# Counts of an edge loop: windows of 128 targets in place of spans of 256-target blocks

## What is computed

```python
# layer 0: a message for each edge, summed by its source
m = jnp.concatenate([x[row], x[col]], axis=1)
m = jax.nn.relu(m @ Wm1 + bm1)
m = jax.nn.relu(m @ Wm2 + bm2)
m_sum = jax.ops.segment_sum(m, row, num_segments=x.shape[0])
...
# layer 2: the mean over the first ten edges of each source
keep = (rank < NUM_NEIGHBORS).astype(x.dtype)
sums = jax.ops.segment_sum(x[col_s] * keep[:, None], row_s, num_segments=N)
...
# layer 3: messages scaled by the edge's weight, summed by target
agg = jax.ops.segment_sum(edge_weight[:, None] * x[src], dst, num_segments=N)
```

## Time and profile before

| what | us |
|---|---|
| median of 3 runs | 911.99 |
| lowest and highest of them | 909.75, 913.79 |
| the profiled execution | 920.58 |
| its span, first to last instruction | 918.7 |
| TensorE busy in the span | 851.9 (93%) |
| VectorE busy | 662.7 (72%) |
| ScalarE busy | 503.2 (55%) |
| GpSimd busy | 292.2 (32%) |

### The profile page before, as it was taken

One profiled execution on the slowest core, in us unless ns is written; L12 is line 12 of the kernel. 1 busy time (PEld: TensorE's weight loads), 2 busy tenths in 40 slices (PEclk: granted clock), 3 DMA queues, 4 the chain that ended last, 5 costly groups with the idle time before them and its releaser, 6 DMA issues.

```text
span 918.7 us, 18692 instructions
## 1 busy us (share of the span) xinstructions
PE 851.9 (93%) x5480; PEld 545.4 (59%) x5514; DVE 662.7 (72%) x1786; ACT 503.2 (55%) x1009; POOL 292.2 (32%) x403
## 2 busy tenths in 40 slices
PE   8899949999999999999999898899899998899898
PEld 3657728989898989898889645322242223232244
DVE  6999985767766767777677466977587776877651
ACT  6432114666656666666666674566656665566531
POOL 8040047556555556555555200012031110111000
PEclk9999979999999999999999999999999999999999
DMA  3020041121212121212122100000000000000310
GB/s 87 32 87 1 0 139 60 54 69 46 69 51 70 51 69 51 68 53 70 46 71 54 47 1 1 0 1 1 1 0 1 1 1 0 1 1 0 128 57 23
DMA packets 19145, 35.87 MB, mean 39 GB/s; under 512 B 5280, under 2 KB 11552, under 8 KB 18976
## 3 DMA queue, kind: packets, MB, share of 16 engines
q0 software_dynamic: 7104, 19.41, 7.5%
q1 hardware_dynamic: 12000, 15.95, 5.1%
HBM read 29.56 MB, written 5.79 MB: 38 GB/s over the span
## 4 chain that ended last, share of the span: by engine, by line
PE 77%; DVE 15%; ACT 4%; issue 3%; POOL 1%; DMA 0%; DVEq 0%; ACTq 0%; POOLq 0%
PE PS L1453 9%; PE PS L1309 8%; PE PS L1223 7%; PE PS L1222 7%; PE PS L1170 5%; PE PS L1438 5%; PE PS L1303 5%; PE PS L1241 5%; DVE OHd L1005 5%; PE PS L1444 4%; PE PS L1215 3%; PE PS L1353 3%; PE PS L1228 3%; PE PS L1404 2%; PE PS L1300 2%
## 5 line engine op out<-in xcount | busy, mean ns | idle before, releaser
L406 POOL DMA_INDIRECT room<-Qtab,gidx x148 | 148.3, 1002 | 96.0 <-DVE gidx L837 61.2
L556 ACT ACTIVATE OHe<-OHs,sew 128x128 bf16<-128x128 bf16 x408 | 126.7, 390 | 46.6 <-DVE OHs L947 26.2
L1005 DVE CUSTOM_DVE_ANT_0 OHd<-PS,room 128x1024 bf16<-128x1024 f32 x96 | 112.3, 1220 | 8.6 <-PE PS L1404 8.5
L420 POOL TENSOR_SCALAR KV<-room,pid 128x256 bf16<-128x256 uint8 x74 | 74.9, 1012 | 134.5 <-DVE MS L912 128.8
L567 ACT ACTIVATE m2s<-m2s 128x512 f32<-128x512 f32 x68 | 42.9, 631 | 88.2 <-DVE m2s L938 60.3
L458 POOL TENSOR_TENSOR zl<-AL,Sx 128x8 f32<-128x8 f32 x9 | 1.9, 215 | 265.1 <-DVE Sx L1005 265.1
L1222 PE MATMUL PS<-Wm,m1T 128*128 128x256 f32 x276 | 83.2, 383 | 0.0
L1223 PE MATMUL PS<-Wm,m1T 128*128 128x256 f32 x276 | 82.8, 382 | 0.0
L952 DVE TENSOR_SCALAR OHd<-iotaN,dstf 128x1024 bf16<-128x1024 f16 x136 | 74.3, 586 | 9.3 <-PE PS L1309 9.3
L912 DVE TENSOR_TENSOR MS<-PS,room 128x512 f32<-128x512 f32 x68 | 47.1, 692 | 43.1 <-PE PS L1241 42.8
L938 DVE TENSOR_TENSOR m2s<-PS,bm 128x512 f32<-128x512 f32 x68 | 47.0, 691 | 42.7 <-PE PS L1223 42.7
(11 more groups left out here) (357 smaller groups left out, 1734.4 us busy)
## 6 DMA issues: line engine op xcount, KB each, us to landing
BT<-Wtab SPq DMA_DIRECT2D x1, 4096.0 KB, 13.1
room<-Qtab,gidx POOLq DMA_INDIRECT x148
room<-Stab SPq DMA_DIRECT2D x1, 2048.0 KB
Wtab<-H SPq DMA_DIRECT2D x4, 512.0 KB, 3.8
Wtab<-cs SPq DMA_DIRECT2D x4, 512.0 KB, 3.4
Qtab<-room SPq DMA_DIRECT2D x1, 1024.0 KB, 4.4
Wn<-in_L_gnn_Wn SPq DMA_DIRECT2D x1, 1024.0 KB, 5.4
x<-in_x SPq DMA_DIRECT2D x1, 512.0 KB, 4.0
```

Source lines behind the costliest of these rows:

```text
L406: g.indirect_dma_start(out=G[:, p % SLOTS, k, :], out_offset=None, in_=Qtab, in_offset=bass.IndirectOffsetOnAxis(ap=gidx[:, p, k:k + 1], a ...
L556: a.activation(OHe[:, k, j, :], OHs[:, k, :], ACT.Copy, scale=sew[:, j, bass.ds(2 * g + k, 1)])
L1005: v.tensor_tensor_reduce(junk[n % 2], bank(4, 2), mask[:, i, :], 1.0, 2 * FAR, ALU.subtract, ALU.max, Sx[:, i, hd:hd + 1]).then_inc(S("gat ...
```

## The change

Each chunk of a pair gets a window of its own, 128 targets wide, whose first target is a multiple of 32 and which lies wholly in one half (512 targets) of the nodes. A pass then has two chunks k by one window by 1 + 3 matmuls: 8 in place of 16. Where a chunk's targets don't fit into such a window, both chunks of the pair go through the same aligned windows of 128, in as many passes as it takes. The number read for a pair now packs the source block, the place of each chunk's window in steps of 32 (five bits each), and the number of further passes (three bits). The loop variable counts targets; the second chunk's window lies `further` beyond the first's.

The places come out of the least and the greatest target of each chunk. VectorE writes them into `rngp` (target + 1, zero where there is no edge) and `sew0` (target - 1024), TensorE turns both with four transposes into bank 6 (72 pairs down, 128 edges across), VectorE takes the maximum and the minimum over the edges, works out places, wide pairs and passes in nineteen small steps on 72 x 2 values, TensorE turns the packed numbers into one row (bank 4), and one VectorE addition with GpSimd's `pblk` makes `rngi`. All but that last addition now stand ahead of the first message. TensorE's wait for `spans` moves from inside the pair loop to ahead of the first `restarted()`. Allocations are left out of the diff.

```diff
@@ -36,6 +36,8 @@
 SLOPE = 0.2
 FRAC = 1.0 / 1024.0
 HALF = 65536.0
+STEP = 32
+PLACES = N // STEP
 FAR = -1e30
 BANK = 512
 
...
@@ -393,7 +399,7 @@
-            g.tensor_scalar(pblk[:, 1, 0:NPAIR - 2], pblk[:, 0, 2:NPAIR], float(NB * NB), None, ALU.mult)
+            g.tensor_scalar(pblk[:, 1, 0:NPAIR - 2], pblk[:, 0, 2:NPAIR], float(PLACES * PLACES * NB), None, ALU.mult)
...
@@ -843,13 +848,10 @@
             link(v.tensor_copy(srcl[:], ssrc[:]))
             link(v.scalar_tensor_tensor(srcl[:], srcl[:], 1.0, valid[:], ALU.add, ALU.mult))
             v.tensor_scalar(srcl[:], srcl[:], -1.0, None, ALU.add).then_inc(S("sources_ready"), 1)
-            v.tensor_copy(paired(dstf), sdst)
-            link(v.tensor_scalar(paired(skey), sdst, 7, None, ALU.arith_shift_right))
-            link(v.tensor_copy(sew0[:], skey[:]))
-            link(v.scalar_tensor_tensor(rngp[:], sew0[:], 1.0, valid[:], ALU.add, ALU.mult))
-            v.tensor_tensor(inblk, rngp[:].unsqueeze(1).to_broadcast([P, NB, NCH]),
-                            iota[:, 1:NB + 1].unsqueeze(2).to_broadcast([P, NB, NCH]), ALU.is_equal)\
-                .then_inc(S("blocks_marked"), 1)
+            link(v.tensor_copy(paired(dstf), sdst))
+            v.scalar_tensor_tensor(rngp[:], dstf[:], 1.0, valid[:], ALU.add, ALU.mult)
+            v.scalar_tensor_tensor(sew0[:], dstf[:], float(-N), valid[:], ALU.add, ALU.mult)\
+                .then_inc(S("ends_marked"), 1)
 
             eng.wait_ge(S("sources_ready"), 1)
             for k in range(2):
@@ -866,39 +868,38 @@
                     link(v.tensor_tensor(sewv[:], sewv[:], sew[:, k, :], ALU.subtract))
             v.tensor_copy(rank[:], sew[:, 0, 0:2]).then_inc(S("weights_split"), 1)
             made = bank(5).rearrange("p (k f) -> p k f", k=2)
-            eng.wait_ge(S("blocks_counted"), 1)
-            held = bank(6, 2)[0:FEW, :].rearrange("p (u n) -> p u n", u=2)[:, :, 0:NB // 2 * NPAIR]\
-                .rearrange("p u (b g) -> p u b g", g=NPAIR)
-            for i, rank_of in enumerate((falling[0:FEW, :], iota[0:FEW, 1:NB + 1])):
-                last = v.scalar_tensor_tensor(flags.rearrange("p (u b) g -> p u b g", u=2), held, 1.0,
-                                              rank_of.unsqueeze(2).to_broadcast([FEW, NB, NPAIR])
-                                              .rearrange("p (u b) g -> p u b g", u=2), ALU.min, ALU.mult)
-                if i:
-                    last.then_inc(S("blocks_read"), 1)
-                    eng.wait_ge(S("blocks_read"), 1)
-                else:
-                    link(last)
-                link(v.tensor_reduce(rngf[:, i, :], flags.rearrange("p b g -> p g b"), AX.X, ALU.max))
+            eng.wait_ge(S("ends_across"), 1)
+            ends = bank(6)[0:NPAIR, :].rearrange("p (u k e) -> p u k e", u=2, k=2)
+            v.tensor_reduce(above[:], ends[:, 0], AX.X, ALU.max)
+            v.tensor_reduce(below[:], ends[:, 1], AX.X, ALU.min).then_inc(S("ends_read"), 1)
+            eng.wait_ge(S("ends_read"), 1)
+            link(v.tensor_scalar(least[:], below[:], float(N), float(N - 1), ALU.add, ALU.min))
+            v.tensor_scalar(steps[:], least[:], 5, None, ALU.arith_shift_right)
+            link(v.tensor_scalar(upper[:], least[:], 9, None, ALU.arith_shift_right))
+            link(v.tensor_scalar(other[:], upper[:], float(BANK // STEP), float((BANK - P) // STEP), ALU.mult, ALU.add))
+            link(v.tensor_tensor(place[:], steps[:], other[:], ALU.min))
+            link(v.scalar_tensor_tensor(other[:], place[:], float(-STEP), above[:], ALU.mult, ALU.add))
+            link(v.tensor_tensor(wide[:], other[:, 0:1], other[:, 1:2], ALU.max))
+            v.tensor_scalar(wide[:], wide[:], float(P), None, ALU.is_gt)
+            link(v.tensor_tensor(upper[:, 0:1], least[:, 0:1], least[:, 1:2], ALU.min))
+            link(v.tensor_scalar(upper[:, 1:2], upper[:, 0:1], 7, None, ALU.arith_shift_right))
+            link(v.tensor_tensor(above[:, 0:1], above[:, 0:1], above[:, 1:2], ALU.max))
+            link(v.scalar_tensor_tensor(above[:, 1:2], upper[:, 1:2], float(-P), above[:, 0:1], ALU.mult, ALU.add))
+            link(v.tensor_scalar(steps[:, 0:1], above[:, 1:2], float(P - 1), None, ALU.add))
+            link(v.tensor_scalar(steps[:, 1:2], steps[:, 0:1], 7, None, ALU.arith_shift_right))
+            v.scalar_tensor_tensor(below[:, 0:1], steps[:, 1:2], -1.0, wide[:], ALU.add, ALU.mult)
+            link(v.scalar_tensor_tensor(other[:], upper[:, 1:2].to_broadcast([NPAIR, 2]), float(P // STEP), place[:],
+                                        ALU.mult, ALU.subtract))
+            link(v.scalar_tensor_tensor(place[:], other[:], wide[:, 0:1], place[:], ALU.mult, ALU.add))
+            link(v.scalar_tensor_tensor(below[:, 1:2], place[:, 1:2], float(PLACES), place[:, 0:1], ALU.mult, ALU.add))
+            v.scalar_tensor_tensor(packed[:], below[:, 1:2], float(NB), below[:, 0:1], ALU.mult, ALU.add)\
+                .then_inc(S("packed"), 1)
             eng.wait_ge(S("gathered"), 1)
             eng.wait_ge(S("pparts_done"), 1)
             v.tensor_tensor(MS[:], made, G[:, 0, :, :], ALU.add).then_inc(S("msg_ready"), 1)
-            link(v.tensor_scalar(rngf[:, 1, :], rngf[:, 1, :], 1.0, -1.0, ALU.max, ALU.add))
-            link(v.tensor_scalar(rngf[:, 0, :], rngf[:, 0, :], -1.0, float(NB), ALU.mult, ALU.add))
-
-            link(v.tensor_tensor(rngf[:, 0, :], rngf[:, 0, :], rngf[:, 1, :], ALU.min))
-            link(v.tensor_tensor(rngf[:, 1, :], rngf[:, 1, :], rngf[:, 0, :], ALU.subtract))
-            link(v.tensor_scalar(rngf[:, 1, :], rngf[:, 1, :], 2.0, None, ALU.add))
-            link(v.tensor_copy(rngi[:], rngf[:, 1, :]))
-            link(v.tensor_scalar(rngi[:], rngi[:], 1, None, ALU.arith_shift_right))
-            link(v.tensor_copy(rngf[:, 1, :], rngi[:]))
-            link(v.tensor_scalar(nfrom[:], rngf[:, 1, :], -2.0, float(NB), ALU.mult, ALU.add))
-            link(v.tensor_tensor(nfrom[:], nfrom[:], rngf[:, 0, :], ALU.min))
-            link(v.tensor_scalar(rngf[:, 1, :], rngf[:, 1, :], 2.0, -1.0, ALU.mult, ALU.add))
-            link(v.tensor_tensor(rngf[:, 1, :], rngf[:, 1, :], nfrom[:], ALU.add))
             eng.wait_ge(S("pair_blocks"), 1)
-            link(v.tensor_tensor(rngf[:, 1, :], rngf[:, 1, :], pblk[:, 1, :], ALU.add))
-            v.scalar_tensor_tensor(rngi[:], nfrom[:], float(NB), rngf[:, 1, :], ALU.mult, ALU.add)\
-                .then_inc(S("spans"), 1)
+            eng.wait_ge(S("packed_across"), 1)
+            v.tensor_tensor(rngi[:], bank(4)[0:1, 0:NPAIR], pblk[0:1, 1, :], ALU.add).then_inc(S("spans"), 1)
 
 
             rankb = bank(4)[:, F2:2 * F2]
@@ -1244,18 +1245,19 @@
                 last.then_inc(S("pparts_done"), 1)
 
             eng.wait_ge(S("sources_across"), 1)
-            eng.wait_ge(S("blocks_marked"), 1)
-            for u in range(2):
-                marks = inblk[:, u * NB // 2:(u + 1) * NB // 2, :].rearrange("p b (g k) -> p b g k", k=2)
+            eng.wait_ge(S("ends_marked"), 1)
+            for u, end in enumerate((rngp, sew0)):
                 for k in range(2):
-                    last = t.matmul(bank(6 + u)[0:FEW, 0:NB // 2 * NPAIR], onesb[:, 0:FEW], marks[:, :, :, k],
-                                    start=(k == 0), stop=(k == 1))
-            last.then_inc(S("blocks_counted"), 1)
+                    at = (2 * u + k) * P
+                    last = t.transpose(bank(6)[0:NPAIR, at:at + P], paired(end)[:, :, k], ident[:])
+            last.then_inc(S("ends_across"), 1)
 
             t.sem_inc(S("pair_done"), 1)
             t.sem_inc(S("ranks_done"), 1)
             t.sem_inc(S("counts_added"), 1)
-            eng.wait_ge(S("blocks_read"), 1)
+            eng.wait_ge(S("ends_read"), 1)
+            eng.wait_ge(S("packed"), 1)
+            t.transpose(bank(4)[0:1, 0:NPAIR], packed[:], ident[0:NPAIR, 0:NPAIR]).then_inc(S("packed_across"), 1)
             eng.wait_ge(S("P_parts"), 3)
             eng.wait_ge(S("turned_onehots"), 1)
             sources(0, 0)
@@ -1277,13 +1279,15 @@
             layers(0)
             g0, end = 0, last_pair(eng, 0)
             eng.wait_ge(S("src_onehots"), 1)
+            eng.wait_ge(S("spans"), 1)
             restarted()
             for b in range(NB):
                 with eng.Fori(g0, end) as g:
-                    eng.wait_ge(S("spans"), 1)
-                    span = eng.value_load(rngi[0:1, bass.ds(g, 1)], min_val=1, max_val=NB * NB * NB - 1)
-                    slot, first = eng.snap((g + 2) & (SLOTS - 1)), eng.snap((span >> 6) & (NB - 1))
-                    least, past = eng.snap((span >> 3) & 7), eng.snap((span & 7) + 1)
+                    span = eng.value_load(rngi[0:1, bass.ds(g, 1)], min_val=0, max_val=PLACES * PLACES * NB * NB - 1)
+                    slot, first = eng.snap((g + 2) & (SLOTS - 1)), eng.snap((span >> 13) & (NB - 1))
+                    near = eng.snap((span << 2) & (N - STEP))
```

(35 more changed lines are left out.)

## The result

| | before | after |
|---|---|---|
| median, us | 912.23 (909.75 to 915.38, 8 runs) | 917.39 (915.39 to 920.31, 8 runs) |
| profiled execution, us | 920.58 | 915.83 |
| its span, us | 918.7 | 914.0 |
| TensorE busy in that span, us | 851.9 (93%) | 837.2 (92%) |
| matmuls of the counts | 1136 | 616 |

The kernel became slower by a ratio of 1.006 (95% interval 1.0043 to 1.0077), some 5 us. The two profiled executions say the opposite, 4.7 us in favour of the change. That contradiction is the key to this case: the profiled execution of before lay 8.3 us above the median in the table (8.6 above the median of three that the prediction had), and above every one of the 31 other runs of that kernel in this study, of which the longest took 915.38. What it showed in excess was not the kernel's usual way.

What follows compares the result with a forecast made beforehand. Bound taken to be the m2s path and a VectorE-POOL ring, not TensorE's matmuls. Terms -0.8 + 9.0 + 0.8 - 0.5 = +8.5 us on the median 911.99 gave 920.5 us, own range 914 to 926, with rivals 912 to 930.

Steps and rivals of the forecast that it cites:

- further passes: Counts loop: 9 extra passes in place of 3, each 1.4 + 0.1 us, +9.0 us (2.7 to 10.2).
- ordinary pairs: One-pass pairs: only some three early in each block gain about 0.1 us, -0.8 us in all (-4.3 to 0).
- changes of block: First pairs of the eight blocks: no sequencer lead, so 0.1 us more each shows, +0.8 us (-2.4 to +2.4).
- ahead of the loop: Before the pair loop: VectorE steps swapped, second message sooner, -0.5 us (-1.1 to +0.5).
- the rival's sum: Shorter ordinary pairs, -6 to -11 us, beside +9.3 us for the other terms: 910 to 915 us.
- the second ring: Later pairs of a block: VectorE, POOL's gathers, a late signal, VectorE; 5.08 us a round, untouched by the counts.
- late signal: L1241's semaphore to VectorE's L912 falls 0.5 to 0.6 us after POOL's second gather, whenever L1241 ends near it.
- m2s: Bias and relu path to L1309 takes 1.41 us, so fewer counts bring L1309 forward by 0.18 us at most.
- the ring gives way: Rival: the signal misses the gather, about 60 pairs shorten by 0.1 to 0.18 us, 910 to 915 us; chance 0.22.
- the round of L912: Sign in the profile after: from one VectorE L912 to the next, 5.0 to 5.1 us.
- The sequencer: Rival: added sums of 0.35 us or more a pass put TensorE's sequencer behind, 3 to 20 us on top; chance 0.10.
- TensorE as the bound: Rival: freed 0.445 us shortens every pair, about 883 us, or 902 for a third of it; chance 0.08.

Runs made afterwards that it cites:

- e1: The kernel before, run and traced once more with no edit: 909.78 us (one run).
- e3: The kernel after with no pair ever taken for wide, 68 passes in place of 77, some edges uncounted: 904.59 us, 0.9915 of before.
- e4: The kernel after with each matmul of the counts issued twice, 16 in a pass, 77 passes: 919.96 us, 1.009 of before.
- e5: The kernel after with the first pass written straight and the loop entered only for further windows, computing the same: 905.42 us, 0.9922 of before.
- e6: The kernel after with the second chunk counted in the first one's window, so the sums for `further` go: 908.74 us, 0.9957 of before.
- e2: The kernel before with the second 256-target half of each pass left out, 8 matmuls in each of 71 passes: 901.73 us, ratio 0.9886.
- e7: The kernel after with ScalarE's relu on m2s done for the first chunk only: 918.27 us (one run).

## Why the prediction was right, and where it was not

Forecast +8.5 us, 920.5; measured 917.39, +5.2 (912.23 to 917.39), inside the forecast's own range of 914 to 926, on the side foreseen. The loss, its place and its size for the passes were foreseen; that the total came out within 3.3 us owes something to luck, as the terms show. By its terms, with e1 as the trace of before:

| term | forecast, us | measured, us |
|---|---|---|
| further passes | +9.0 | +9.0: nine cost 12.8 after, three cost 3.8 in e1 |
| ordinary pairs | -0.8 | -4.2 over 60 pairs, from 5.01 to 4.94 in the mean |
| changes of block | +0.8 | +0.4 (50.29 against 49.92 for seven) |
| ahead of the loop | -0.5 | -0.5 in these two traces, to the first L1309 from the same VectorE instruction (`srcl`) on: 24.40 to 23.87; other traces disagree, see below |
| sum | +8.5 | +4.7 in the traces, +5.2 in the times |

*The passes* came as forecast: 77 of them, at 1.38 to 1.50 us for one (pair 21's two 2.86). e3 shows that they are the whole loss, e4 that it isn't their matmuls, e5 and e6 that it is the register work and the loop around them. The +9.0 is closer than its parts. The 1.40 for a pass of before came from the odd execution, where e1 has 1.25 to 1.28; the 1.5 foreseen for one of after was 1.43 in the mean; and nine at 1.5 less three at 1.4 would have been 9.3, which the rival's sum uses. Nor was the 0.1 more that of added instructions: a further pass has ten of them before and after. Six of the seven two-pass pairs took 6.32 to 6.39 us, just under the 6.4 that was to show the forecast, and pair 21 7.80.

*The step that failed is the second ring,* and with it the term of -0.8 for the ordinary pairs, which were -4.2. That the matmuls bring "nothing for one in the POOL ring" was read from pairs of the profiled execution in which L912 came late, and these pairs are not how the kernel runs otherwise: e1 shows none of them. With it fell the reason to give the gain of 0.1 us to three pairs in a block only. All 60 have a gain, but it is smaller than the 0.1 to 0.18 that I allowed, since without the late signal m2s is only 0.06 us ahead of TensorE. The prediction had the warning in hand, 8.6 us between the profiled run and the median, and carried the periods over unscaled all the same. In effect the rival "the ring gives way" came true for ordinary pairs, at two thirds of its smallest gain, together with the forecast's price for the passes; its own range, 910 to 915, was missed. The range's upper end, 926, lies above the 925.1 that all upper ends at once would give.

*m2s* is the part that held best: L1313 1.40 us behind L939 against 1.41 forecast, and 4.94 us in e2, e3, e5 and e6, whatever else was changed. The waits of 0.2 to 0.35 us that it was to show are there, 0.35 in pair 11; the round of L912, foreseen at 5.0 to 5.1 us, is 4.94 like the pair's.

*The sequencer* was a rival with a threshold of 0.3 us of lead, for which the prediction names no row. The lead was smaller, 0.16 us in e1 and 0.06 after: e7 shows the sequencer at 4.94 already, level with m2s. It costs ordinary pairs nothing only because m2s ends at the same point, and for the same reason hardly any part of a further pass is covered. e5 has that cover.

*TensorE as the bound* is out for the kernel after (e2, e7) and true for the kernel before by 0.06 us a pair (e1), which is all that 0.445 us of freed work brought. The Trainium skill, "Perfetto Trace Analysis", section "Identifying the Most-Contended Engine", says to work on the engine with the highest occupancy first, and to judge TensorE's headroom by the share of peak rate that its matmuls reach and by the busy share of its weight loads. Here TensorE was busy for 98% of the loop and its weight loads for 87%. Taken as a promise that 520 matmuls at 55.6 ns give back their 28.9 us, the rule misleads: the gain in ordinary pairs was 4.2 us.

*Ahead of the loop*, `packed` was ready 1.4 us before the sources could start, so nothing was lost there, and the second message came 0.96 us sooner behind the first (bound 1.1). The times can't show 0.5 us: from trace to trace the first turned one-hots begin 8.2 to 11.0 us after `srcl`. That the term agrees to the tenth is luck. From `srcl` to the first L1309 the three traces with the old code ahead of the loop take 23.60 to 24.69 us, and the seven with the new code beside that of after 24.25 to 26.12. In those seven the load of the sources' row (`room<-Stab`), which the first turned one-hots wait for, is issued 4.5 to 5.9 us after `srcl`, in the old code and in after 3.4 to 3.7. So the new code may cost time there rather than save it; why the load is issued later no run shows.

## What to carry to other kernels

Compare the profiled execution with the median of the runs before reading periods from it, and where they differ by more than the effect that is sought, take a second trace. Before removing work from an engine that looks full, measure in one round how much earlier the next path is ready: here 0.06 us, and that was all that 0.445 us of freed work brought. In a short loop with a trip count from data, the sequencer's register work and closing branch can be the price of a pass (1.4 us around 0.445 us of matmuls); count its instructions, and see how far the sequencer is ahead of the array. Here fewer sums in the pass gave most of the gain (e6), and writing the common single pass straight, with the loop kept for the rare rest, gave all of it and computes the same (e5).

## What the runs showed of the hardware

A further pass of the counts loop cost 1.25 to 1.28 us with 16 matmuls (e1) and 1.38 to 1.50 with 8 (after), each with ten instructions of TensorE's sequencer. Those for registers come about one every 0.1 to 0.17 us in the trace of after, though an ALU_OP itself is shown with 36 ns:

```profile
L1299 PEldq ALU_OP  x290: 36/36/40, 141.8 to 502.6; - x145
L1299 PEldq FUSED_REGOPS  x154: 68/84/121, 142.1 to 502.7; - x154
L1299 PEldq COMPARE_BRANCH  x77: 67/76/209, 143.3 to 502.9; - x77
```

The closing branch takes 67 to 82 ns in the 68 records where the loop ends and 208 or 209 in the nine where it goes round. The Trainium skill, "Runtime: NRT & Kernel Launch", section "Instruction fetch mechanics", states that a taken branch whose target lies outside the current window of instructions stalls on a fetch, and that this is one reason why control flow at run time is dear. No run here shows whether this loop's start lies outside that window, so the 209 ns speak neither for it nor against.

In one execution of the kernel before, in 46 of 68 pairs, and hardly once in any of the other traces, the semaphore of a matmul came up to 0.44 us later than usual when it was due within about 0.5 us behind a gather's end on GpSimd. In the other traces it is due as near, as a rule 0.44 us behind it in e1 and 0.39 after, and comes on time. Its cause is open.

Ahead of the loop, GpSimd's second gather takes 2.03 to 2.04 us in the three traces with the old code, which has VectorE's marks beside it, and 1.14 to 1.15 in the eight without them; that the marks are the reason is not shown.
